# Fused field attention on one core: loading x and storing y two groups of the batch at a time

## What is computed

```python
q = (jnp.einsum('bfe,oe->bfo', x, Wq) + bq).reshape(B, F, H, D)
k = (jnp.einsum('bfe,oe->bfo', x, Wk) + bk).reshape(B, F, H, D)
v = (jnp.einsum('bfe,oe->bfo', x, Wv) + bv).reshape(B, F, H, D)
scale = 1.0 / jnp.sqrt(jnp.float32(E))
att = jnp.einsum('bfhd,bghd->bhfg', q, k) * scale
att = jax.nn.softmax(att, axis=-1)
out = jnp.einsum('bhfg,bghd->bfhd', att, v).reshape(B, F, H * D)
res = jnp.einsum('bfe,oe->bfo', x, Wr) + br
return jax.nn.relu(out + res)
```

## Time and profile before

| | |
|---|---|
| median of 3 executions | 938.09 us (936.63 to 940.19) |
| the profiled execution, its own time | 944.5 us |
| its span, first to last instruction | 942.4 us |
| TensorE's mean granted clock in it | 0.995 |
| PE busy / POOL / ACT / DVE | 97% / 93% / 82% / 77% of the span |
| DMA traffic | 101.20 MB, mean 107 GB/s |

### The profile page before, as it was taken

One profiled execution on the slowest core, in us unless ns is written; L12 is line 12 of the kernel. 1 busy time (PEld: TensorE's weight loads), 2 busy tenths in 40 slices (PEclk: granted clock), 3 DMA queues, 4 the chain that ended last, 5 costly groups with the idle time before them and its releaser, 6 DMA issues.

```text
span 942.4 us, 68912 instructions
## 1 busy us (share of the span) xinstructions
PE 916.0 (97%) x30720; PEld 680.3 (72%) x30720; DVE 726.7 (77%) x2066; ACT 769.2 (82%) x1541; POOL 876.5 (93%) x1028
## 2 busy tenths in 40 slices
PE   6999999999999999999999999999999999999996
PEld 4777777777777777777777777777777777777774
DVE  6777777778777877777777777777778777777775
ACT  4888888888887888878888788887888888888885
POOL 3999999999998999989999999999999999999997
PEclk9999999999999999999999999999999999999997
DMA  4333333333333333333333333333333333333321
GB/s 117 100 108 109 108 115 110 109 110 115 108 107 105 109 109 108 110 104 107 116 108 110 108 109 114 112 109 102 115 109 109 114 105 116 109 109 106 108 77 65
DMA packets 67433, 101.20 MB, mean 107 GB/s; under 512 B 13632, under 2 KB 46656, under 8 KB 67136
## 3 DMA queue, kind: packets, MB, share of 16 engines
q1 hardware_dynamic: 66704, 96.65, 33.7%
q10 hardware_dynamic: 432, 0.15, 0.1%
HBM read 54.81 MB, written 41.94 MB: 103 GB/s over the span
## 4 chain that ended last, share of the span: by engine, by line
PE 97%; issue 2%; ACT 0%; DMA 0%; DVE 0%; POOL 0%; POOLq 0%; ACTq 0%
PE vr_bank L429 24%; PE o_bank L461 22%; PE s_buf L402 19%; PE o_bank L382 14%; PE s_buf L438 10%; PE vr_bank L419 6%; PE vr_bank L431 1%; DMA biases<-bias_in 0%; PE o_bank L386 0%; POOL y_sum L187 0%; ACT rv L254 0%; ACT y_rows L234 0%; POOLq L35 0%; ACT q_flat L227 0%; PE vr_bank L424 0%
## 5 line engine op out<-in xcount | busy, mean ns | idle before, releaser
L179 POOL TENSOR_TENSOR m_diag<-m_split,ident 128x640 bf16<-128x640 bf16 x256 | 322.2, 1258 | 49.7 <-DVE m_split L332 35.2
L187 POOL TENSOR_TENSOR y_sum<-rv,y_att 128x512 f32<-128x512 f32 x256 | 302.9, 1183 | 1.9 <-DVE y_att L343 1.9
L195 POOL TENSOR_SCALAR q_bd<-q_flat,consts 128x320 f32<-128x320 f32 x512 | 265.8, 532 | 10.8 <-DVE kT L316 10.8
L431 PE MATMUL vr_bank<-w_cols,xT 64*128 64x128 f32 x2048 | 270.9, 273 | 0.0
L429 PE MATMUL vr_bank<-w_cols,xT 64*128 64x128 f32 x2048 | 270.7, 273 | 0.0
L254 ACT ACTIVATE rv<-vr_bank 128x1024 f32<-128x1024 f32 x256 | 260.1, 1016 | 0.0
L321 DVE TRANSPOSE_TENSOR_REDUCE s_buf<-s_buf 128x20 f32<-128x640 f32 x256 | 221.5, 865 | 46.2 <-PE s_buf L402 46.2
L429 PEld LDWEIGHTS vr_bank<-w_cols,xT 64*128 64x128 f32 x2048 | 251.2, 190 | 0.0
L431 PEld LDWEIGHTS vr_bank<-w_cols,xT 64*128 64x128 f32 x2048 | 250.4, 189 | 0.0
L461 PE MATMUL o_bank<-rv,pT 64*40 64x33 f32 x16384 | 225.0, 202 | 10.3 <-issue 8.3
L402 PEld LDWEIGHTS s_buf<-q_bd,kT 64*40 64x40 f32 x8192 | 150.9, 112 | 116.0 <-issue 115.0
(11 more groups left out here) (33 smaller groups left out, 624.1 us busy)
## 6 DMA issues: line engine op xcount, KB each, us to landing
xT<-xT_in SPq DMA_DIRECT2D x512, 104.0 KB, 2.5
y<-y_rows SPq DMA_DIRECT2D x512, 80.0 KB
w_cols<-w_in SPq DMA_DIRECT2D x1, 128.0 KB, 2.2
vr_bias<-vr_bias_in ACTq DMA_DIRECT2D x1, 128.0 KB, 3.4
consts<-consts_in ACTq DMA_DIRECT2D x1, 20.0 KB, 2.0
biases<-bias_in ACTq DMA_DIRECT2D x1, 1.0 KB, 3.7
```

The source lines that it names most:

```text
L179: pool.tensor_tensor(m_diag[:], m_split[:, place % 2].unsqueeze(2).to_broadcast([P, BLOCKS, QUAD]), ident[:].unsqueeze(1).to_broadcast([P, ...
L187: pool.tensor_tensor(y_sum[:, n % 3].rearrange("r (a d) -> r a d", d=DIM), rv[:, place % 4, 1, :, 0:DIM], y_att[:, place % 2].rearrange("r ...
L195: pool.tensor_scalar(q_bd[:, place % 4, :, s], q_flat[:, place % 2].rearrange("d (b f) -> d b f", f=FIELDS), consts[:, C_HEAD + s:C_HEAD + ...
L431: mm = nc.tensor.matmul(vr_bank[:, 1, OUT * pair:OUT * (pair + 1)], xT[HALF:P, place % 8, cols], w_cols[HALF:P, 1], start=False, stop=True ...
```

## The change

Two neighbouring groups travel together. The host lays the rows of two groups side by side, so that a row of x is 832 floats (3328 bytes) and a row of y 1024 floats (4096 bytes). `xT` becomes 4 buffers of two groups in place of 8 of one, and `y_rows` 4 buffers of two groups in place of 4 of one. SP issues four transfers in two turns, each twice as large: 512 loads and 512 stores become 256 and 256. The total of bytes stays. The two lanes of one pair of groups are loaded one turn apart, and the two halves of a pair of y are stored nearly two turns apart.

```diff
-            def load(n, place, lane):
-                sp.dma_start(xT[lane:lane + HALF, place % 8, 0:PAD], xT_in[n, lane:lane + HALF]).then_inc(x_loaded[place % 8], 16)
+            def load(two, lane):
+                sp.dma_start(xT[lane:lane + HALF, two % 4, 0:TWO * PAD], xT_in[two, lane:lane + HALF])\
+                    .then_inc(x_loaded[two % 4], 16)
+
+            for two in range(4):
+                load(two, 0)
+                load(two, HALF)
+
+            def store(two, g):
                 if g == 0:
-                    sp.wait_ge(y_ready, n + 1)
-                sp.dma_start(out[n, g], y_rows[HALF * g:HALF * g + FIELDS, place % 4]).then_inc(y_stored[place % 4], 16)
+                    sp.wait_ge(y_ready, TWO * (two + 1))
+                sp.dma_start(out[two, g], y_rows[HALF * g:HALF * g + FIELDS, two % 4].rearrange("r t c -> r (t c)"))\
+                    .then_inc(y_stored[two % 4], 16)
+
+            def two_groups(two):
+
+                n = TWO * two
+                if two > 0 and exists(n + 6):
+                    sp.wait_ge(vr_made, n + 1)
+                    load(two + 3, HALF)
+                if two > 2:
+                    store(two - 3, 0)
                 if exists(n + 8):
+                    sp.wait_ge(vr_made, n + 2)
+                    load(two + 4, 0)
+                if two > 2:
+
+                    sp.wait_ge(shifted, n + 1)
+                    store(two - 3, 1)
+
+            for two in range(STEPS // TWO):
+                two_groups(two)
+            for two in range(STEPS // TWO - 3, STEPS // TWO):
+                store(two, 0)
+                store(two, 1)
...
             def relu(n, place):
-                if not before(n, 4):
-                    act.wait_ge(y_stored[place % 4], 32 * (turn_of(n, place, 4) - 1))
+                if n % TWO == 0 and n >= 8:
+                    act.wait_ge(y_stored[n // TWO % 4], 32 * (n // 8))
                 act.wait_ge(sum_ready, n + 1)
-                nc.scalar.activation(y_rows[:, place % 4], y_sum[:, n % 3], ACT.Relu).then_inc(y_ready, 1)
+                nc.scalar.activation(y_rows[:, n // TWO % 4, n % TWO], y_sum[:, n % 3], ACT.Relu).then_inc(y_ready, 1)
...
-                if exists(n + 1):
-
-                    pe.wait_ge(x_loaded[(place + 1) % 8], 32 * turn_of(n + 1, place + 1, 8))
+                if exists(n + 1) and (n + 1) % TWO == 0:
+
+                    pe.wait_ge(x_loaded[(n + 1) // TWO % 4], 32 * ((n + 1) // 8 + 1))
```

More of the change, by code:

```diff
@@ L86, in attention_kernel @@
         set_up = sem("set_up")
-        x_loaded = [sem(f"x_loaded{i}") for i in range(8)]
+        x_loaded = [sem(f"x_loaded{i}") for i in range(4)]
         qk_made = sem("qk_made")
@@ L132, in _ @@
             sp.dma_start(w_cols[:], w_in).then_inc(weights, 16)
-            def load(n, place, lane):
-                sp.dma_start(xT[lane:lane + HALF, place % 8, 0:PAD], xT_in[n, lane:lane + HALF]).then_inc(x_loaded[place % 8], 16)
[L137 to L144, removed]
-                if g == 0:
-                    sp.wait_ge(y_ready, n + 1)
-                sp.dma_start(out[n, g], y_rows[HALF * g:HALF * g + FIELDS, place % 4]).then_inc(y_stored[place % 4], 16)
@@ L149, in group @@
-            def group(n, place):
-                if exists(n + 8):
[L152 to L169, removed]
+            def load(two, lane):
[5 more added lines that the diff above has]
+            def store(two, g):
+                if g == 0:
+                    sp.wait_ge(y_ready, TWO * (two + 1))
+                sp.dma_start(out[two, g], y_rows[HALF * g:HALF * g + FIELDS, two % 4].rearrange("r t c -> r (t c)"))\
+                    .then_inc(y_stored[two % 4], 16)
@@ L170, in _ @@
+            for two in range(STEPS // TWO):
[3 more added lines that the diff above has]
+                store(two, 1)
             for place in range(4):
-                sp.wait_ge(y_stored[place], 32 * (STEPS // 4))
+                sp.wait_ge(y_stored[place], 32 * (STEPS // TWO // 4))
         @block.gpsimd
@@ L369, in tokens @@
             def tokens(place, lane):
-                x = xT[lane:lane + HALF, place % 8]
+                x = xT[lane:lane + HALF, place // TWO % 4, place % TWO * PAD:]
                 return bass.AP(x.tensor, x.offset, [x.ap[0], [PAIR, SLOTS], [HALF, 2], [1, FIELDS]])
@@ L427, in values_and_residual @@
                 for pair in range(SLOTS):
-                    cols = slice(PAIR * pair, PAIR * pair + P)
-                    nc.tensor.matmul(vr_bank[:, 0, OUT * pair:OUT * (pair + 1)], xT[0:HALF, place % 8, cols],
+                    cols = slice(place % TWO * PAD + PAIR * pair, place % TWO * PAD + PAIR * pair + P)
+                    nc.tensor.matmul(vr_bank[:, 0, OUT * pair:OUT * (pair + 1)], xT[0:HALF, place // TWO % 4, cols],
                                      w_cols[0:HALF, 1], start=False, stop=True, skip_group_check=True)
-                    mm = nc.tensor.matmul(vr_bank[:, 1, OUT * pair:OUT * (pair + 1)], xT[HALF:P, place % 8, cols],
+                    mm = nc.tensor.matmul(vr_bank[:, 1, OUT * pair:OUT * (pair + 1)], xT[HALF:P, place // TWO % 4, cols],
                                           w_cols[HALF:P, 1], start=False, stop=True, skip_group_check=True)
@@ L513 @@
     arrays = {
-        "xT_in": xT.reshape(steps, P, PAD),
+        "xT_in": np.ascontiguousarray(xT.reshape(steps // TWO, TWO, P, PAD).transpose(0, 2, 1, 3)).reshape(steps // TWO, P, TWO * PAD),
         "w_in": np.ascontiguousarray(np.stack([np.concatenate([Wq.T, Wk.T]), np.concatenate([Wv.T, Wr.T])], 1)),
@@ L522 @@
             for name, a in arrays.items()]
-    args.append(nc.dram_tensor("y", (steps, 2, FIELDS, SLOTS * OUT), _mybir.dt.float32, kind="ExternalOutput").ap())
+    args.append(nc.dram_tensor("y", (steps // TWO, 2, FIELDS, TWO * SLOTS * OUT), _mybir.dt.float32, kind="ExternalOutput").ap())
     attention_kernel(nc, *args)
     r = run_bass_kernel_spmd(nc, [arrays], core_ids=[0])
-    rows = r.results[0]["y"].reshape(steps, 2, FIELDS, MEMBERS, 2, OUT)
+    rows = r.results[0]["y"].reshape(steps // TWO, 2, FIELDS, TWO, SLOTS * OUT).transpose(0, 3, 1, 2, 4)
+    rows = rows.reshape(steps, 2, FIELDS, MEMBERS, 2, OUT)
     y = np.empty((steps, 2, 2, MEMBERS, FIELDS, OUT), np.float32)
```

9 lines of the change are left out of this document (5 added, 4 removed).

## The result

The changed kernel takes 960.32 us (median of 4, 958.15 to 961.18) against 938.58 us for the kernel before (median of 4). The ratio is 1.0229, 95% interval 1.0203 to 1.0255: 21.7 us slower, where I had forecast 0.8 us and given slower a chance of 0.19. The profiled execution took 960.13 us with a span of 957.5 us, against 944.5 and 942.4 for the one of before. So the two profiles show 15.1 us of the difference. The profiled execution of before was slower than the four that its median comes from (936.6 to 940.2 us), so what its profile shows as lost is likely above the usual.

The account below looks back on a forecast made before the run. PE was taken to bound the kernel; four terms of 0, start +0.3 and end +0.5 summed to +0.8 us, added to the 938.09 median for 938.9 us, likeliest case's range 935 to 942, 8 times in 10 931.0 to 945.0.

Parts of the forecast that it names:

- What bounds the kernel: Whole span: PE binds, 97% busy; only the middle's 25.2 us, read as instruction-fetch stops, can be touched outside start and end.
- Fewer transfers on SP: SP's queue: halving the transfers relieves SP of some 256 us, but it idled 321 us and nobody waited; 0.
- pairs in time: Loads and stores of pairs: x keeps 14.7 us of slack, stores over 14 us, so no wait is added; 0.
- The order on SP: SP's queue: a store, load and store follow closely every second turn; transfers behind have over 14 us of slack; 0.
- The middle's 25.2 us: Time lost over 244 turns to stops without semaphore waits; change taken as 0, bounded by -25.2 and 5.0 us.
- my two cases: Fetch at 277.4, quiet engines, followed by a stop; fetch at 328.1, busy engines, followed by none; taken as data mattering little.
- the price for the rival: Middle's fetches: each met at chance 0.337, waits half a transfer, 0.05 us becoming 0.10; at most 12.5 us, cut to 5.0.
- The slower rival: Middle: longer rows and three close transfers starve the instruction fetch; 5.0 us, 12.5 at most, giving 943.9 us; chance 0.17.
- The faster rival: Middle: fewer moments of traffic let fetches find quieter engines; a third of 25.2 us goes, giving 930.5 us; chance 0.13.
- The start: Chain through the `biases` transfer, which may land later by nothing or 0.6 us beside doubled first loads; middle taken, +0.3 us.
- the 1.0 us of cover: Start: x may come 1.0 us later before anyone sees it, hiding the first two loads' extra 0.6 us.
- The end: Last two stores behind the last ReLU carry two groups each, 0.3 us more if overlapping, 0.6 if not; +0.5 us.

Follow-up runs that it names:

- e4: The kernel before without steady traffic: x of the first 8 groups serves all, only the last 4 groups are stored; 928.3 us, ratio 0.9899.
- e5: Changed kernel's two-group transfers, but one load and directly behind it one store every turn, begun when the turn's attend is done; 945.8 us, ratio 1.0079 to the kernel before.
- e6: Changed kernel's two-group transfers, one load and one store every turn, begun at the turn's end without the waits on `o_made`; 964.2 us, ratio 1.0260 to the kernel before.
- e1: Changed kernel with the same transfers and schedule, but short rows of 1664 and 2048 bytes again; 960.1 us, ratio 1.0245 to the kernel before.
- e2: Changed kernel with each store waiting for the next attend, about half a turn away from the load; 947.5 us, ratio 1.0106 to the kernel before.

## Why the prediction was wrong

*What bounds the kernel: right.* PE is the bound, and traffic touches it only in the stops. These are instruction fetches, as I had argued, and they come every 256 instructions, not every turn.

*Fewer transfers on SP and pairs in time, each 0: right.* PE's only wait for x is still the first, and SP only waits more. *The order on SP, 0:* right in that no later transfer was needed sooner, but it left out what the order does to the fetches.

*"The middle's 25.2 us: I take 0": this is the step that failed.* It measured +12.7 us in the profile, and the longer stops of TensorE at its block boundaries are what it measured. The median moved by more. Three things were wrong with it. First, I judged by two fetches with engines busy or quiet beside them. A fetch that shares the time with data isn't held up much: it takes 1.08 us on average without traffic (e4), 1.14 in the kernel before and 1.11 in the changed one. What differs is when it begins, and neither of my two windows looked at the time before the fetch. There my two cases say the opposite. The "quiet" fetch began at 277.44, 1.47 us after the boundary at 275.98, and data had 44% of the engines' time between; the "busy" one began at 328.19, only 0.85 us after the boundary at 327.34, with 15% between. Second, I took "the order changes" for harmless because nobody waits for x or y. The moved place is the larger part: e5 and e6 differ by 1.8% through it alone, while e5, with double transfers in a better place, is only 0.8% above the kernel before. Third, the price for the rival, half of one transfer (0.155 us before, 0.31 after), was that of a single transfer met at random. The burst of a load and a store that follow each other was about 1.9 us long (288.0 to 289.9), and it came at the same moment of every second turn.

*The slower rival: the right mechanism in part, and mis-sized.* I gave it 5.0 us, 12.5 at most; the profile's middle has 12.7 and the median 21.7 with the ends. It had the bursts and the three transfers close together, but priced neither the place nor the sum, and of its two causes the longer rows do nothing (e1). The Trainium skill's page "DMA: Bandwidth & Descriptors", section "Queues, rings and completion order", speaks of whole packets of several descriptors; I read it as one row. e1 rules the single row out. The long stop, whose fetch began when a whole load and a whole store had passed, does not contradict the page read rightly, but no row here shows where such a packet ends.

My sentence that by the Trainium skill's page no transfer of data could change the middle went further than the page's "mostly hidden", and the runs speak against it.

*The faster rival: wrong for this order*, though traffic does lengthen the stops (e4, ratio 0.9899). After the change a turn has fewer moments of traffic, but they fell where they cost more (e2 and e5 against the changed kernel and e6).

*The start, +0.3: mis-sized, it measured +1.7* (turn 4 at 22.62 against 20.89). Both parts of the chain moved. The biases took 5.04 us in place of 3.68, and x came at 7.48 in place of 5.73. The changed kernel's rows, chain and timeline:

```profile
1.64 5.04 DMA biases<-bias_in
```

```profile
7.48 0.87 PE L382 MATMUL o_bank<-xT,w_cols 64*128 64x320 f32 x1 [7.48 <-DMA xT<-xT_in]
```

x at 7.48 is 1.75 us later than before, more than the 1.0 us of cover that I had named. SP's first two loads, from issue to landing (min/median/max, the window of the first 2.2 us):

```profile
DMA to landing us min/median/max: 4.7/5.1/5.5
```

I had given a double load 2.8 us. At the start it needs 4.7 and 5.5, beside the loads of the weights and constants and those that SP issues next.

*The end, +0.5: half of what it measured, +1.0.* The last ReLU ends at 953.26 + 0.63 = 953.89, and the span at 957.5, 3.6 us later where it was 2.6:

```profile
953.26 0.63 ACT L234 ACTIVATE y_rows<-y_sum 128x512 f32<-128x512 f32 x1 [2.32 <-POOL y_sum L187]
```

*What stays open.* The profiled executions differ by 15.1 us, the medians by 21.7; the rest lies in executions without a trace. Why the fetch alone still costs some us with quiet engines (e4) wasn't tried. That a fetch waits in a queue behind data isn't shown: it is read from its late start and from what place and density do, and no row shows the queue itself. Data can't be the only reason for a late start either, since e4, without them, has 13 stops of 0.15 to 0.43 us, whose fetches began 1.33 us after the boundary. On average the fetches begin 1.07 us after it in both kernels; the change made the latest ones later, not all of them.

## What to carry to other kernels

When an engine is busy 97% of the time and hardly waits for a semaphore, compare its undisturbed turn with its average one: what makes the difference may be the fetch of its own instructions. TensorE here needs a block of 16.4 KB about once a turn, which comes by DMA as the data do, so the moment at which transfers go out was worth up to 2% here, even though each of them had 14 us of slack. Before merging transfers or moving them in such a kernel, look at what the DMA engines do just before each instruction fetch, and count transfers that are issued back to back as one burst.

## What the runs showed of the hardware

TensorE's stops stand exactly 256 of its instructions apart (128 matmuls and 128 weight loads), and the gaps at these places make up nearly all of what the middle loses: 25.4 us beside a loss of 25.2 in the kernel before and 38.3 beside 37.9 in the changed one, some 3 us of each sum being ordinary gaps. In these two traces PE passes such a place 1.2 us or more after the end of a block's fetch. A fetch takes about as long beside data (1.11 to 1.14 us on average) as without them (1.08); before long stops it begins later (1.81 us after the boundary, 0.88 where there is no stop). With steady traffic the middle loses 25.2 us over 244 turns, without it 6.1, one execution each; the medians on one chip differ by 7.5 us. The same bytes in the same transfers cost 18.4 us more at the end of a turn than behind the attend. Rows of 1664 or 3328 bytes make no difference at equal transfers (960.1 and 960.3 us, ratios 1.0245 and 1.0229).
